# Metaformer block (token pruning, merging, top-k attention, mixture of experts): attention's rows put back by token number, and the projection stage rewritten

## The reference, cut to what matters

```
x  = x + cam(ln(x));  t = tokens(x);  out = t + ffn(ln(t))

cam(xf):                                            # per image, N = 3136
  gt = mean(xf) @ W_gt;  score = (xf @ W_k) . gt    # one number a token
  reserve = the 1568 tokens of highest probability, in order of rank
  x_res = xf[reserve];  src, dst = x_res[::2], x_res[1::2]      # 784 each
  best match of each src among dst (cosine of x @ W_k)
  the 471 best matched src are averaged into their dst, 313 stay
  x_merge = [313 unmerged src, 784 merged dst] -> 1097 rows
  8 heads: softmax over the 137 largest of 1097 scores per row, times v
  restored: dst rows as they are, src rows: their own, or their dst's
  full[reserve] = restored; tokens not in reserve keep xf
  return full @ W_proj + b_proj

ffn(h):                                             # all 50176 tokens
  probs = softmax(h @ gate_w + gate_b), idx = argmax, prb = its value
  pos = place of the token in its expert's queue (cumulative count)
  tokens up to the capacity: (relu(h @ w1[idx] + b1) @ w2[idx] + b2) * prb
```

## Time and profile before

| | |
|---|---|
| median of 3 runs | 12841.58 us (12824.29 to 12856.08) |
| the profiled execution: time, span | 12803.12 us, 12801.4 us |
| mean granted TensorE clock | 0.637 of full speed |
| busy over the span: PE, DVE, ACT, POOL | 8366.2, 9275.5, 7022.4, 2257.8 us |
| indirect DMAs of POOL in rank, project, experts | 448, 1008, 560 |

### The profile page before, as it was taken

The page is one execution under the profiler, slowest core; times in us unless marked ns, Lnnn a source line. Parts: engine busy times, 40 slices in busy tenths (PEclk is TensorE's granted clock), DMA queues, the critical chain, the costliest instruction groups (busy, mean ns, idle before and its releaser), DMA issues. The chain is left out here.

```text
span 12801.4 us, 168034 instructions
## 1 busy us (share of the span) xinstructions
PE 8366.2 (65%) x45969; PEld 5441.5 (43%) x45969; DVE 9275.5 (72%) x26008; ACT 7022.4 (55%) x11609; POOL 2257.8 (18%) x2136
## 2 busy tenths in 40 slices
PE   4555577774767666767775777766677653333699
PEld 4555455552434333334443444433344323333587
DVE  8999534436989888889998999988889882222243
ACT  0000021124979777889997999977799751111232
POOL 2333211110000000000000000000000005777676
PEclk9999855555656655666665666655566555555555
DMA  2222000000000000000000000000000002222221
GB/s 68 58 60 62 18 22 19 18 20 15 14 11 15 11 12 12 13 13 15 15 15 12 15 15 15 15 12 12 12 15 15 12 7 48 58 58 55 52 57 43
DMA packets 561347, 330.83 MB, mean 26 GB/s; under 512 B 463685, under 2 KB 498212, under 8 KB 556820
## 3 DMA queue, kind: packets, MB, share of 16 engines
q1 hardware_dynamic: 493844, 223.42, 7.9%
q0 software_dynamic: 64512, 63.74, 2.0%
q10 hardware_dynamic: 2048, 32.62, 0.7%
HBM read 200.05 MB, written 130.17 MB: 26 GB/s over the span
## 5 line engine op out<-in xcount | busy, mean ns | idle before, releaser
L1021 PE MATMUL a_psT<-a_qt,a_kt 74*122 74x366 bf16 x3456 | 1549.1, 448 | 797.7 <-ACT a_pT L1101 557.4
L1245 DVE TENSOR_SCALAR_CACHE_REDUCE a_s<-a_psS 122x512 f32<-122x512 f32 (+1 forms) x2304 | 1606.8, 728 | 418.7 <-PE a_psS L1004 275.0
L1109 ACT ACTIVATE a_junk<-a_s,a_aim 122x1097 bf16<-122x1097 f32 x1152 | 1383.5, 1208 | 819.3 <-DVE a_s L1245 816.6
L1179 DVE MAX8 a_near<-a_below 122x8 f32<-122x274 f32 (+1 forms) x4608 | 1699.3, 430 | 0.1
L1101 ACT ACTIVATE a_pT<-a_psT 122x732 f32<-122x732 f32 (+1 forms) x1920 | 1369.9, 714 | 590.7 <-PE a_psT L1024 587.6
L1024 PEld LDWEIGHTS a_psT<-a_weigh,a_drops 122*122 122x122 bf16 x10368 | 1565.5, 190 | 190.5
L1172 DVE SCALAR_TENSOR_TENSOR a_below<-a_s,a_te,a_signs 122x1097 f32<-122x1097 f32 x1152 | 1546.6, 1352 | 128.2 <-remote 127.6
L1024 PE MATMUL a_psT<-a_weigh,a_drops 122*122 122x122 bf16 x10368 | 1522.7, 273 | 0.0
L1415 POOL DMA_INDIRECT p_src<-o,p_gi x112 | 104.5, 933 | 7693.5 <-DVE p_ri L1523 7659.6
L1037 PE MATMUL a_psO<-a_pT,a_v 122*32 122x366 f32 x6912 | 1413.3, 704 | 0.0
L1109 ACT ACTIVATE a_signs<-a_s,a_te 122x1097 bf16<-122x1097 f32 x1152 | 1400.8, 1219 | 4.4 <-DVE a_te L1164 4.4
(11 more groups left out here) (342 smaller groups left out, 14659.5 us busy)
## 6 DMA issues: line engine op xcount, KB each, us to landing
xbuf<-r_blank ACTq DMA_DIRECT2D x16, 1990.6 KB, 8.2
e_xg<-xbuf SPq DMA_DIRECT2D x56, 568.8 KB
r_bc<-pr SPq DMA_DIRECT2D x16, 1372.0 KB, 7.0
a_k<-kT SPq DMA_DIRECT2D x384, 51.5 KB
a_q<-qT SPq DMA_DIRECT2D x384, 51.5 KB
a_kt<-kT SPq DMA_DIRECT2D x384, 51.5 KB
a_qt<-qT SPq DMA_DIRECT2D x384, 51.5 KB
r_xt<-in_x SPq DMA_DIRECT2D x16, 784.0 KB
```

Source lines behind the costliest of these rows:

```text
L1021: pe.matmul(out[:, x, 0:CW], kt[q][:, u * QP:(u + 1) * QP], qt[q][:, c * CW:(c + 1) * CW], start=True, stop=False)
L1109: act.activation(out[:, :], s_[:, t, :], ACT.Sign, bias=at[:, t:t + 1], scale=-1.0, accum_out=total[:, t:t + 1]).then_inc(counted[r], 1)
L1179: mx = dve.max(near[:, t, g, :], below[t % 3][:, EDGES[g]:EDGES[g + 1]])
L1245: dve.tensor_scalar(sc[o][:, t, a:b], psS[0:QP, a:b], 1.0, None, ALU.mult, ALU.max, accum_out=peaks[:, i, t:t + 1]).then_inc(evacuated, 1)
```

## The change

Rows are kept in the order of tokens, in a new DRAM tensor `y`.

- *constants*: the projection's and the gate's weights and biases are no longer loaded here (four loads).
- *rank*: rows of `xs` have a 65th column, the token number, which DVE writes with two short instructions before the normalised rows. `ranks` is gone. SP stores the normalised batch to `y` in token order (784 KB a batch); DVE waits for that store (`laid`) before it overwrites the tiles. ACT clears `o` at the start with three DMAs, 4.5 MB in all.
- *merge*: SP loads the kept rows in two DMAs (sources, destinations) of 256-byte pieces, and the token numbers in two more, of 4-byte pieces (`own`). POOL converts the numbers to `k.tokens` before its copy of the sources.
- *attend*: POOL gets a program. For batches 0 to 14, once the heads are stored, it runs `place`: a direct load of the destination rows, 7 gathers of source rows from `o`, and 14 scatters into `y` by token number.
- *project*: `place` runs for batch 15 only, and there are no other gathers. SP loads `y` and x. The order is unrolled: PE turns and projects batch b+2 between the gate of b and its counts; tiles are turned in pairs, and the products are made from rows 0 to 63 and 64 to 127 in turn. The projection's bias is added to x by POOL (`bias`, one instruction a batch), the gate's by DVE. Rows to be sent have three buffers; t has its own two, and ACT copies it into the row. The store of x + attention goes out as soon as the sum is there.

```
 # rank, DVE
-                dve.tensor_tensor(xls[u][:, :, :], xc[:, :, :], rs.unsqueeze(2)...
+                link.then(dve.tensor_scalar(xls[u][:, :, C], k.tok[:, :], k.doff[0:TP, :], None, ALU.add))
+                link.then(dve.tensor_scalar(k.doff[:, :], k.doff[:, :], float(N), None, ALU.add))
+                dve.tensor_tensor(xls[u][:, :, 0:C], xc[:, :, :], rs.unsqueeze(2)...
 ...
+                            dve.wait_ge(laid[1 - u], 16 * (i + u))
 ...
-                link.then(dve.tensor_copy(k.ranks[:, bass.ds(b * NT, NT)], cnt[:, 1, :]))
 # merge, SP
+                for h in range(2):
+                    sp.dma_start(sd[:, :, h * C:(h + 1) * C], kept[:, :, h, 0:C]).then_inc(rows_in, 16)
+                for h in range(2):
+                    sp.dma_start(own[:, :, h:h + 1], kept[:, :, h, C:C + 1], allow_slow_non_contiguous=True).then_inc(own_in, 16)
 # attend
+        @block.gpsimd
+        def _(pool):
+            for b in range(B - 1):
+                pool.wait_ge(o_stored, 16 * (H // 2) * (b + 1))
+                place(pool, k, d, b, b, srcs, dsts, src_in, dst_in, put)
+def place(pool, k, d, b, n, srcs, dsts, src_in, dst_in, put):
+    pool.dma_start(dsts[:, :, :], d.o[b * MP:b * MP + ND, :].rearrange("(i p) c -> p i c", p=TP)).then_inc(dst_in, 16)
+    for i in range(NS):
+        pool.indirect_dma_start(out=srcs[:, i, :], ... in_=d.o, ... ap=k.gidx[:, b * NS + i:b * NS + i + 1] ...
+    pool.wait_ge(dst_in, 16 * (n + 1))
+    for i in range(NS):
+        pool.indirect_dma_start(out=d.y, ... ap=k.tokens[:, b, i, 1:2] ... in_=dsts[:, i, :] ...
+    pool.wait_ge(src_in, 16 * NS * (n + 1))
+    for i in range(NS):
+        pool.indirect_dma_start(out=d.y, ... ap=k.tokens[:, b, i, 0:1] ... in_=srcs[:, i, :] ...
+    pool.wait_ge(put, 16 * 2 * NS * (n + 1))
 # project, SP
+            for b in range(B):
+                sp.wait_ge(x2_made, 4 * (b + 1))
+                sp.dma_start(tiles(d.out, b), tw[b % 3][:, :, C:2 * C]).then_inc(stored[b % 3], 16)
+                if b + 2 < B:
+                    load(b + 2)
 # project, POOL
-    (gathers of sources, gathers by rank)
+            bias(0)
+            bias(1)
+            place(pool, k, d, B - 1, 0, srcs, dsts, src_in, dst_in, put)
+            for b in range(B):
+                if b + 2 < B:
+                    bias(b + 2)
+                pool.wait_ge(placed, b + 1)
+                pool.wait_ge(laid, b + 1)
                 for j in range(NT):
+                    pool.indirect_dma_start(out=d.xbuf, ... ap=sis[b % 2][:, j:j + 1] ... in_=tw[b % 3][:, j, :] ...
 # project, PE
+            attended(0)
+            attended(1)
+            for b in range(B):
+                routed(b)
+                if b + 2 < B:
+                    attended(b + 2)
+                tally(b)
 # project, ACT
+            for b in range(B):
+                for q in range(NQ):
+                    take(tT, t_turn(b), q)
+                    if q == 1 and b + 1 < B:
+                        square(b + 1)
+                if b + 1 < B:
+                    root_(b + 1)
+                if b + 2 < B:
+                    for q in range(NQ):
+                        take(yT, y_turn(b + 2), q)
+                act.wait_ge(shifted, b + 1)
+                act.activation(pe_[:, :, :], lg[:, :, :], ACT.Exp).then_inc(exped, 1)
+                act.wait_ge(normed, b + 1)
+                act.activation(tw[b % 3][:, :, 0:C], ts[b % 2][:, :, :], ACT.Copy).then_inc(laid, 1)
 # project, DVE
+            normalise(0)
+            for b in range(B):
+                if b + 1 < B:
+                    normalise(b + 1)
+                choose(b)
+                seat(b)
```

More of the change, by code:

```diff
@@ L732, in _ @@
             with pool.Fori(0, B) as b:
-                pool.wait_ge(rows_in, 16 * b + 16)
+                pool.wait_ge(own_in, 32 * b + 32)
+                apart(pool, k)
+                pool.tensor_copy(k.tokens[:, bass.ds(b, 1), :, :].rearrange("p a i two -> p (a i two)"),
+                                 own[:, :, :].rearrange("p i two -> p (i two)"))
+                pool.wait_ge(rows_in, 32 * b + 32)
                 apart(pool, k)
@@ L1361, in project @@
         psP = ps("p_psP", [TP, 4, 512])
[L1362 to L1367, removed]
@@ L1368, in project @@
-        src_in, dst_put, src_put, y_in, x_in, sent, stored = ([sem(f"p_{x}{u}") for u in range(2)] for x in (
-            "src_in", "dst_put", "src_put", "y_in", "x_in", "sent", "stored"))
-        block = ctx.enter_context(nc.Block())
[L1371 to L1383, removed]
+        psL = [ps(f"p_psL{h}", [TP, 512]) for h in range(2)]
@@ L1395, in body, with load @@
[L1395 to L1407 removed]
+            def load(b):
+                u = b % 2
+                if b == B - 1:
+                    sp.wait_ge(put, 16 * 2 * NS)
+                sp.dma_start(ys[u][:, :, :], tiles(d.y, b)).then_inc(y_in[u], 16)
+                sp.dma_start(xts[u][:, :, :], tiles(d.x, b)).then_inc(x_in[u], 16)
@@ L1443, in _, with bias @@
-            for u in range(2):
-                sources(0, u)
-            gather(0, 0)
-            batches(pool, body)
-            for u in range(2):
-                pool.wait_ge(sent[u], 16 * NT * (B // 2))
+            def bias(b):
+                u = b % 2
+                pool.wait_ge(x_in[u], 16 * (b // 2 + 1))
+                pool.tensor_tensor(xts[u][:, :, :], xts[u][:, :, :], bproj[:, :].unsqueeze(1).to_broadcast([TP, NT, C]),
+                                   ALU.add).then_inc(biased, 1)
@@ L1450, in _ @@
+            for u in range(3):
+                pool.wait_ge(sent[u], 16 * NT * len(range(u, B, 3)))
         @block.tensor
         def _(pe):
[L1452 to L1460 removed]
@@ new lines, in attended @@
+            def attended(b):
+                pe.wait_ge(y_in[b % 2], 16 * (b // 2 + 1))
+                turn(ys[b % 2], y_turn(b))
+                if b:
+                    pe.wait_ge(x2_made, 4 * b)
+                for r in range(NT // 2):
+                    for h in range(2):
+                        mm = pe.matmul(psP[:, 2 * h + r // HERE, r % HERE * C:(r % HERE + 1) * C],
+                                       yT[h * C:(h + 1) * C, r * TP:(r + 1) * TP], wproj[h * C:(h + 1) * C, :],
+                                       start=True, stop=True)
@@ L1590, in body @@
                 link.then(dve.tensor_tensor(df, df, dump, ALU.add))
+                if b >= 2:
+                    dve.wait_ge(sent[(b - 2) % 3], 16 * NT * ((b - 2) // 3 + 1))
                 dve.tensor_copy(si[:, :], df).then_inc(placed, 1)
-                link.then(dve.tensor_scalar(k.doff[:, :], k.doff[:, :], float(N), None, ALU.add))
-                dve.wait_ge(placed, b + 1)
-                apart(dve, k)
-                link.clear()
-            batches(dve, body)
+            dve.wait_ge(loaded, 16 * 6)
+            normalise(0)
[4 more added lines that the diff above has]
+                seat(b)
+            link.all()
+            link.clear()
 def experts(nc, k, d):
```

289 lines of the change are left out of this document (143 added, 146 removed).

## The result

The changed kernel takes 12234.27 us (median of 4 runs, 12221.7 to 12279.9), the kernel before beside it 12848.76 us (median of 4 runs, 12824.29 to 12856.08): ratio 0.9536, 95% interval 0.952 to 0.9552, faster. The forecast was 12230. The profiled execution took 12231.48 us, its span 12229.6 us.

A forecast was written before the change was run, and what follows sets the result against it. POOL's 63 indirect DMAs per batch, one behind the other, were taken to bound project. Project -627, rank +7, merge +2, attention +10 and start loads -1 took 12803 to 12194 us, 12230 as median (0.3% above); range 12140 to 12340.

The forecast's parts named there:

- POOL is the bound of project: Project stage: POOL's indirect DMAs set its time, so fewer save 627 us, giving 12230 us; 76%.
- The period: Project, POOL's time per batch: 28 scatters at 1.242 us, 2.9 us of stalls and 3.7 for the bias, 41.4 us.
- The bias: Project: one added POOL tensor_tensor over 112x1792 per batch, 3.54 us at merge's 1.97 ns a column, plus 0.2 wait.
- Stalls: Project: POOL scatters held by DVE instructions with two SBUF inputs, 2.9 us a batch, ends 1.4 and 4.4.
- The start: Project's beginning: scatters begin at 10689, when seat(0) ends; POOL is done with bias(2) at 10685; ends -10 to +10.
- The chain: Project's DVE, PE and ACT work per batch: 31 us, hidden behind 37.7 us of scatters; as rival bound 12295, 10%.
- Rank: Rank stage: two short DVE instructions more per batch, +7 us, ends +3 and +7; other waits counted as 0.
- sign of being wrong: Rank: L494, DVE's wait for scatters (22.4 us in 7 batches before), waiting longer would show the prediction wrong.
- Merge: Merge stage: loads in two pieces and 4-byte tokens show only in batch 0, +2 us, ends 0 and +5.
- Attention: Attention stage: POOL's 15 `place` runs cost DVE's short steps +10 us, ends -10 to +73.
- DVE not held: Attention: POOL's DMAs don't hold DVE's two-input instructions; the rival that they do, +31 to +83 us, had 9%.
- The sum: Whole kernel: 12803 - 627 + 7 + 2 + 10 - 1 = 12194 us profiled, 12230 as median by the 0.3% ratio.

The follow-up runs named there:

- e1: Adds 28 gathers a batch, into a spare tile nobody reads, to POOL in the changed kernel's project stage; 12796.41 us, ratio 0.997.
- e4: Changed kernel with POOL also adding a tile of zeros after the bias, so the bias costs twice; 12298.24 us, ratio 0.9575.
- e2: Adds two unused DVE reductions of 2.02 us a batch, ahead of the indices, to the changed kernel; 12237.03 us, ratio 0.9534.
- e3: Adds six unused DVE reductions, 12.2 us a batch, ahead of the indices, to the changed kernel; 12252.96 us, ratio 0.9542.
- e9: No edit: the kernel before, profiled a second time; span 12858.8 us.
- e10: No edit: the kernel before, profiled a third time; span 12841.9 us.
- e11: No edit: the changed kernel, profiled a second time; span 12223.3 us.
- e5: Changed kernel with `place` left out of attention, so attended rows of batches 0 to 14 are missing; 12223.14 us, ratio 0.9519.
- e6: Changed kernel running `place` three times for each of batches 0 to 14; 12245.6 us, ratio 0.9544.
- e7: Changed kernel with the projection's bias moved from POOL to DVE, its vector in PSUM; 12210.36 us, ratio 0.95.
- e12: Changed kernel with project's `mean` and `rs` in PSUM, the bias staying on POOL; 12189.91 us, ratio 0.9488.

## Why the prediction was right, and where it wasn't

**POOL is the bound of project** (76%): right. e1 and e4 move the time by what they add to POOL, e2 adds as much as e4 to DVE and leaves the period alone. For the stage -627 us was forecast and -624.6 measured between the first profiles.

**The period**, 41.4 us forecast, 41.57 measured, from these terms. The bias: 3.54 forecast, 3.97 measured. I took its rate from a merge instruction over 64 partitions whose second input is bf16 in the kernel; the one here goes over 112 and reads a float32 vector through a broadcast. Which of these differences makes 2.21 ns a column of 1.97, no run tells. This term was mis-sized by 0.43 x 13 = 6 us. The Trainium skill, GPSIMD Engine Reference, section 3.1, by which I had named an estimated 3.9 us, was nearer; the trace agrees with it within 2%. The gap after the bias was 0.17 us in place of the usual 0.30. Stalls: two a batch, 2.54 and 2.29 us for 0.94, together 2.95 us; 2.9 forecast, from "some 45 us" that are 43 by the forecast's own figures (1292 less 1249), or 2.7 a batch. Scatters from first to last, 646.8 us; forecast 646.

**The start**: first scatter 72.5 us after the last store forecast (10689 less 10616.5), 74.9 measured (10721.3 less 10646.4), and as forecast it was the chain that came last there: POOL was done with `place` and its biases 4.0 us before the indices.

**The chain**: indices at S+30.8 forecast, 29.5 us after DVE's start measured. The 56 gate matmuls took 5.4 us a batch (5.8 forecast), the projection's 5.5 us where they took 8.55. The error lay in what it was set against: the 37.7 us of scatters gave "7 us to spare", though POOL does the bias, too, before it asks for the indices. e3 shows 12 us of room in the steady state, the 8 and the bias's 4, and only the first batch dearer.

**Rank**: +7 forecast, +7.0 measured between the first profiles, +4 to +6 in the other profiles with the change; DVE's wait for the scatters is 25.1 us in 7 batches for 22.4. A longer wait there was named as a sign of being wrong; it is 2.7 us in all. `laid` is in no row of its own:

```profile
DVE r_small L502 <- DMA xs<-r_xl,r_idx: 25.1, 7, 4.0
```

**Merge**: +2 forecast, +4.2 in the first profiles, +1.5 to +4 from e9 and e10 to e11. No wait for the tokens stands out; I have no run that takes this part alone.

**Attention**: +10 forecast, +18.7 measured; `place` costs nothing that e5 and e6 can show, so even my +10 was put down to the wrong thing. What I kept near (DVE not held) was right: L1197 1352 ns, L1323 785 ns, as in the earlier trace rows. What grew is DVE's idle time before it copies the scores, most of it a wait for PE, 418.7 to 445.9 us, at a granted clock of 0.61 and 0.60:

```profile
L1245 DVE TENSOR_SCALAR_CACHE_REDUCE a_s<-a_psS 122x512 f32<-122x512 f32 (+1 forms) x2304 | 1606.8, 728 | 418.7 <-PE a_psS L1004 275.0 <-issue 55.2 <-PE a_psS L993 50.8
L1270 DVE TENSOR_SCALAR_CACHE_REDUCE a_s<-a_psS 122x512 f32<-122x512 f32 (+1 forms) x2304 | 1605.3, 728 | 445.9 <-PE a_psS L1023 310.2 <-PE a_psS L1012 64.5 <-issue 50.9
```

Over the same 7380 us of attention it is 409.7, 420.9 and 423.5 us in the three profiles of before and 436.5 and 431.7 in the two of after.

On both sides of this the Trainium skill speaks in SBUF — State Buffer, section "SBUF: two separate sides": a DVE instruction with two SBUF inputs and a GpSimd one that reads SBUF share a pair of ports, which whoever starts first keeps. The traces bear out the half in which POOL waits (2.54 us, and 0.93 once the input is in PSUM). In the other half, DVE behind an indirect DMA of POOL, no run shows a wait: 2025 ns in project, 1353 ns in attention with 990 DMAs beside it. The same page of the Trainium skill puts the end of such blocking at the DVE instruction's end plus some 115 ns. The rows here can't test this figure: they give only the end of the held scatter as a whole, 0.8 us after DVE's (10964.61 to 10965.41 in e7), where a free one takes 0.93 us in all.

**The sum**: 12194 us was set against a profiled 12803, and 12231 was profiled. The 37 us are 9 of attention, 23 of experts, 2 each of merge and project and 1 of rank with the start. That the forecast of 12230 still came within 4 us of the median 12234 is in part luck. The first profile of before lay 46 us under the median of its kernel, that of after 3 us under its own, and the factor 1.003, by which I carried the one to the other, added 36 us, about what the terms had missed. Against the means of all three profiles of before and both of after the terms themselves fare better: project -625.8, rank +5.8, merge +3.2, attention +7.6, experts +1.6. The spans are 12834.0 and 12226.5 us, 607.6 us apart, and my edits summed to 609. The terms of a few us each are smaller than what the same kernel's stages differ by from one execution to the next, so no profile here confirms them one by one.

## What to carry to other kernels

When one engine issues one indirect DMA after another, count its instructions: 560 of them less at 1.24 us each, with one instruction of 4 us a batch added, make some 640 us by this count, and 625 were measured in the stage. The room that a hidden chain has goes up to the instruction on the bound engine that waits for it, with all that this engine does before (12 us here, where the scatters alone gave 8); the idle time of the chain's own engine in a whole period checks it. And profile the kernel before more than once: stages that no edit touched differed here by 42 us between executions, more than most terms of the sum.

## What the runs showed of the hardware that was not expected

- Moving two small operands (28 numbers a partition each) from SBUF to PSUM freed POOL: scatters 1028 to 942 ns in the mean, 2.8 us a batch (41.57 to 38.75, e12's biases at 10951.12 and 10989.87), with the two DVE instructions as long as before (2.02 us).
- A DVE reduction of the same length with one SBUF input held no scatter: L1589 ran from 10972.52 for 2.02 us in the changed kernel, the scatter of 10972.79 took 0.93 us.
- In the experts' stage the same work took 827.5 to 898.7 us in the 14 profiles, with the granted clock 0.56 at the one end and 0.50 at the other, and three stretches of 31 to 38 us at 0.83 to 0.86 at the one end and none at the other.
